# Mamba and mixture-attention sandwich on one core: the attention stage's value blocks, scores and attention passes put in another order

## What is computed

```python
q = _rope(jnp.einsum('bsd,hdp->bhsp', x, Wq))
k = _rope(jnp.einsum('bsd,hdp->bhsp', x, Wk))
gv = _gate(x, Wsel_v)
v = jnp.einsum('bsd,bhse,hedp->bhsp', x, gv, Wv)
att = jax.nn.softmax(jnp.einsum('bhsp,bhtp->bhst', q, k) / np.sqrt(P), axis=-1)
o = jnp.einsum('bhst,bhtp->bhsp', att, v)
go = _gate(x, Wsel_o)
return jnp.einsum('bhsp,bhse,hepd->bsd', o, go, Wo)
```

## Time and profile before

| what | value |
|---|---|
| median of 3 runs | 4357.75 us (4352.01 to 4357.77) |
| the profiled execution's own time | 4360.78 us |
| its span, first to last instruction | 4358.8 us |
| TensorE busy | 3803.9 us (87%) |
| VectorE busy | 3630.8 us (83%) |
| GpSimd busy | 2849.6 us (65%) |
| ScalarE busy | 2029.6 us (47%) |
| mean granted TensorE clock | 0.909 |

### The profile page before, as it was taken

One profiled execution on the slowest core, in us unless ns is written; L12 is line 12 of the kernel. 1 busy time (PEld: TensorE's weight loads), 2 busy tenths in 40 slices (PEclk: granted clock), 3 DMA queues, 4 the chain that ended last, 5 costly groups with the idle time before them and its releaser, 6 DMA issues. The chain is left out here.

```text
span 4358.8 us, 54031 instructions
## 1 busy us (share of the span) xinstructions
PE 3803.9 (87%) x15744; PEld 2541.1 (58%) x15744; DVE 3630.8 (83%) x4012; ACT 2029.6 (47%) x3761; POOL 2849.6 (65%) x2524
## 2 busy tenths in 40 slices
PE   6777867867765599999999999999999999999787
PEld 2233323323322377777777777777777777777676
DVE  5999999999998478877887887887888788778598
ACT  4544535535443244544444444444444444444433
POOL 2758668567594366766766766766766766766444
PEclk8877877877876799999999999999999999999898
DMA  1000000000000300100100100100100100000101
GB/s 39 0 10 15 24 5 19 24 5 19 15 5 20 131 13 12 41 14 10 41 14 10 41 14 10 41 14 10 41 14 10 41 14 10 20 14 15 31 29 44
DMA packets 48726, 97.83 MB, mean 22 GB/s; under 512 B 3570, under 2 KB 33138, under 8 KB 46228
## 3 DMA queue, kind: packets, MB, share of 16 engines
q1 hardware_dynamic: 47620, 92.94, 6.2%
q0 software_dynamic: 1040, 4.19, 0.2%
HBM read 80.34 MB, written 16.78 MB: 22 GB/s over the span
## 5 line engine op out<-in xcount | busy, mean ns | idle before, releaser
L702 DVE TENSOR_TENSOR_SCAN state<-dA,dBx 128x2048 f32<-128x2048 f32 x128 | 726.8, 5678 | 25.9 <-POOL y_part L289 21.3
L1234 ACT ACTIVATE prob<-ps_b,negmax 128x512 f32<-128x512 f32 x512 | 346.1, 687 | 652.3 <-DVE negmax L1353 652.3
L286 POOL TENSOR_TENSOR state<-state,c_copy 128x1024 f32<-128x1024 f32 x120 | 345.5, 2879 | 374.8 <-DVE state L702 374.8
L1347 DVE TENSOR_TENSOR vg<-ps_b,gates 128x1024 f32<-128x1024 f32 x256 | 313.5, 1224 | 253.1 <-PE ps_b L1072 241.1
L961 POOL TENSOR_TENSOR qk_full<-vg 128x512 f32<-128x512 f32 x256 | 329.0, 1285 | 253.3 <-DVE vg L1347 253.3
L549 ACT ACTIVATE dA<-dt,a_neg 128x511 f32<-128x511 f32 x512 | 326.9, 711 | 323.9 <-DVE state L702 323.7
L974 POOL TENSOR_TENSOR ogT_low<-prob,ogT_high 128x512 fp32r<-128x512 f32 x256 | 324.0, 1295 | 208.9 <-ACT ogT_high L1267 208.9
L372 PE MATMUL ps_a<-xp_high,ident_r 33*128 33x512 f32 x256 | 163.0, 637 | 332.6 <-DVE dBx L692 307.9
L1070 PE MATMUL ps_b<-ogT_high,wo_high 128*128 128x512 f32 x1024 | 413.2, 403 | 11.1 <-DVE ogT_low L1399 10.8
L1070 PE MATMUL ps_b<-wv_high,xT_high 128*128 128x512 f32 x1024 | 414.6, 405 | 0.0
L289 POOL TENSOR_TENSOR y_part<-y_part,state 128x1024 f32<-128x1024 f32 x120 | 403.4, 3362 | 9.4
(11 more groups left out here) (237 smaller groups left out, 9530.9 us busy)
## 6 DMA issues: line engine op xcount, KB each, us to landing
xT<-xT_scratch SPq DMA_DIRECT2D x65, 512.0 KB, 3.3
wv<-in_wv SPq DMA_DIRECT2D x8, 1024.0 KB, 4.9
wo<-in_wo SPq DMA_DIRECT2D x8, 1024.0 KB, 7.0
x_in<-in_x SPq DMA_DIRECT2D x8, 512.0 KB, 4.7
x_a<-in_x SPq DMA_DIRECT2D x8, 512.0 KB, 5.3
x_scratch<-x_a SPq DMA_DIRECT2D x8, 512.0 KB, 2.9
xT_scratch<-x2T SPq DMA_DIRECT2D x8, 512.0 KB, 2.6
scores_scratch<-sg SPq DMA_DIRECT2D x8, 512.0 KB, 3.5
```

Of the source, the lines that this page charges most:

```text
L286: pool.tensor_tensor(state, state, c, ALU.mult).then_inc(hc_part_done, 1)
L702: dve.tensor_tensor_scan(h[n % 2][:, :, :].rearrange("p c s -> p (c s)"), dA[n % 2][:, :, :].rearrange("p c s -> p (c s)"), dBx[n % 2][:, ...
L1234: act.activation(prob[h][:, t, :], ps[:, score_bank(t) + h, :], ACT.Exp, bias=negmax[:, t, h:h + 1], accum_out=total[:, h, t:t + 1]).then_ ...
```

## The change

It does five things in stage B.

1. TensorE: `scores(2)` and `scores(3)` stand ahead of `values(1, 0)`, and `values(1, 3)` stands behind the first head's transposes.
2. TensorE: `attend` makes a head's four passes with the high probabilities first, then its four passes with the low ones. The first four wait for `pT_high` in place of `pT_low`. All eight have 128 columns: `vv` now holds low values, high values and zeros, and the low pass takes the high values and the zeros. `pv_psum` comes from the low passes alone. A wait for the third `gate_values` of the batch is added.
3. VectorE: `gate_values(0)` stands behind `maxima(0)` and `maxima(1)`; `gate_values(3)` behind the first head's `low_probabilities`; `add_parts(0)` behind `low_gates`.
4. `aside` is no longer a tile of its own but the second half of `qk_full`, and `rotate` waits for `oT_done`.
5. GpSimd fills the zeros of `vv` once at the start.

```diff
-        oT, aside = sb("oT", [P, S]), sb("aside", [P, S])
+        oT, aside = sb("oT", [P, S]), qk_full[:, 1, :]
...
-        vv = sb("vv", [P, 2, TT, 2 * HP], F32R)
+        vv = sb("vv", [P, 2, TT, 3 * HP], F32R)
...
             def low_values(it, h):
                 pool.wait_ge(v_high, it * 2 + h + 1)
-                pool.tensor_tensor(vv[:, h, :, HP:2 * HP], v[:, h, :, :], vv[:, h, :, 0:HP].bitcast(F32), ALU.subtract).then_inc(v_low, 1)
+                pool.tensor_tensor(vv[:, h, :, 0:HP], v[:, h, :, :], vv[:, h, :, HP:2 * HP].bitcast(F32), ALU.subtract).then_inc(v_low, 1)
...
             pool.memset(out_gate[:, :, :], 0.0).then_inc(zero_done, 1)
+            pool.memset(vv[:, :, :, 2 * HP:3 * HP].bitcast(F32), 0.0).then_inc(zero_done, 1)
...
-            def attend(it, h, c):
-
-                if c == 0:
-                    pe.wait_ge(v_low, it * 2 + h + 1)
-                n = h * TT + c
-                pe.wait_ge(pT_low, it * N + n + 1)
-                bank, last = ATTEND_BANK[h], c == TT - 1
-                if last:
-                    pe.matmul(ps[0:HP, bank, :], vv[:, h, c, 0:HP], probT[1][:, n % RING, :], start=False, stop=False)
-                mm = pe.matmul(ps[:, bank, :], vv[:, h, c, :], probT[0][:, n % RING, :], start=(c == 0), stop=last)
-                if not last:
-                    mm = pe.matmul(ps[0:HP, bank, :], vv[:, h, c, 0:HP], probT[1][:, n % RING, :], start=False, stop=False)
-                mm.then_inc(pv_psum, 1)
+            def attend(it, h):
+
+                pe.wait_ge(v_low, it * 2 + h + 1)
+                pe.wait_ge(vg_done, it * 4 + 3)
+                bank = ATTEND_BANK[h]
+                for c in range(TT):
+                    pe.wait_ge(pT_high, it * N + h * TT + c + 1)
+                    pe.matmul(ps[:, bank, :], vv[:, h, c, 0:2 * HP], probT[0][:, c % RING, :], start=(c == 0), stop=False)
+                for c in range(TT):
+                    pe.wait_ge(pT_low, it * N + h * TT + c + 1)
+                    pe.matmul(ps[:, bank, :], vv[:, h, c, HP:3 * HP], probT[1][:, c % RING, :], start=False, stop=(c == TT - 1)).then_inc(pv_psum, 1)
...
                 values(it, 0, 3)
-                values(it, 1, 0)
                 scores(it, 2)
                 scores(it, 3)
+                values(it, 1, 0)
                 values(it, 1, 1)
                 values(it, 1, 2)
-                values(it, 1, 3)
                 for n in range(TT):
                     turn_probabilities(it, n)
-                for c in range(TT):
-                    attend(it, 0, c)
+                values(it, 1, 3)
+                attend(it, 0)
                 for n in range(TT, N):
                     turn_probabilities(it, n)
                 turn_gates(it)
-                for c in range(TT):
-                    attend(it, 1, c)
+                attend(it, 1)
...
             def rotate(it):
 
                 dve.wait_ge(vsum_done, CREDIT + it * VSUM)
+                dve.wait_ge(oT_done, it * 2)
...
-                gate_values(it, j, b, 0)
                 maxima(it, 0)
                 maxima(it, 1)
+                gate_values(it, j, b, 0)
                 gate_values(it, j, b, 1)
                 maxima(it, 2)
                 maxima(it, 3)
                 gate_values(it, j, b, 2)
-                gate_values(it, j, b, 3)
                 for n in range(TT):
                     low_probabilities(it, n)
+                gate_values(it, j, b, 3)
                 output_gates(it)
                 if more or more_pairs:
                     tops(*coming, 0)
-                add_parts(it, 0)
                 for n in range(TT, N):
                     low_probabilities(it, n)
                 low_gates(it)
+                add_parts(it, 0)
                 add_parts(it, 1)
```

More of the change, by code:

```diff
@@ L1205, in _ @@
             pe.wait_ge(consts_done, 1)
+            pe.wait_ge(zero_done, 2)
             turns(pe, start, batch)
@@ L1238, in high_values @@
                 act.wait_ge(vsum_done, CREDIT + it * VSUM + h * 6 + 6)
-                act.activation(vv[:, h, :, 0:HP], v[:, h, :, :], ACT.Copy).then_inc(v_high, 1)
+                act.activation(vv[:, h, :, HP:2 * HP], v[:, h, :, :], ACT.Copy).then_inc(v_high, 1)
             def high_probabilities(it, n):
@@ L1472, in _ @@
             dve.wait_ge(consts_done, 1)
-            dve.wait_ge(zero_done, 1)
+            dve.wait_ge(zero_done, 2)
             turns(dve, start, batch)
```

## The result

| | before | changed |
|---|---|---|
| median, same chip | 4354.9 us (4352.01 to 4357.77, 4 runs) | 4574.02 us (4572.49 to 4577.11, 4 runs) |
| span of the profiled execution | 4358.8 us | 4572.0 us |
| its own time | 4360.78 us | 4573.94 us |
| mean granted clock over the span | 0.909 | 0.896 |

The changed kernel is slower by a factor of 1.0504, with a 95% interval of 1.0486 to 1.0522. 4594 was predicted, with a range of 4537 to 4663.

A forecast was written before the change was run, and what follows sets the result against it. TensorE, busy 2516.7 of 2555 us, was taken as the bound, at 40.4 us a batch. Profiled 4360.8 + 211 (batches) + 5 (pair changes) + 20 (clock) - 3 (to the median) = 4594 us, range 4537 to 4663.

The forecast's parts named there:

- Second wait: TensorE before the second head's attention: the late fourth `gate_values` delays sums, `high_values` and rounded blocks; 2.3 us of waiting.
- First wait: TensorE before the first transpose: the last exponential stands behind `high_values(0)`, delayed by the late first `gate_values`; 0.82 us idle.
- rival 1: The wait before the first transpose does not come, as GpSimd's sums run closer together; 2.5 us a batch, 4540 us; chance 0.08.
- Third move: `add_parts(0)` behind `low_gates` holds up `move_part(1)`; `gate_outputs` starts at 3011.59 instead of 3008.28, the output product at 3015.00.
- 3.3 us a batch: Lengthening of each stage B batch, read at the output product's start, 3015.00 instead of 3011.69; 211 us over 64 batches.
- Changes of pair: `low_wqk`, 1.30 us, between the first head's sums delays the first transpose; at most 9 us, less absorbed waits, taken as +5.
- The granted clock: Clock falls in many batches behind the wait before the second head's attention; 0 to 1.1 us a batch, 0.3 taken, 20 us.
- Edits at nothing: Wider low passes, moved scores, later ring freeing, `aside` and `rotate`'s wait, and zeros were taken to cost nothing.
- The sum: Whole kernel: 4360.8 + 211 + 5 + 20 - 3 = 4594 us.
- Rival 2: Clock low for most of the attention, transposes not counting as busy; 147 us in place of 20, 4721 us; chance 0.05.
- Rival 3: Faster: TensorE's own order alone counts, so each batch loses its 1.2 us of waits; 77 us, 4281 us; chance 0.03.
- Rival 4: No change: the new waits just eat the 1.2 us a batch won by grouping; 4358 us; chance 0.01.

The follow-up runs named there:

- e1: The change with `values(1, 3)` back ahead of the first head's transposes and the fourth `gate_values` back ahead of its remainders: 4418.2 us.
- e4: The kernel before with only `values(1, 3)` moved behind the first head's transposes and the fourth `gate_values` behind its remainders: 4551.1 us.
- e2: The change with the first `gate_values` put back ahead of the first two `maxima`: 4528.9 us.
- e3: The change with the first `add_parts` put back ahead of the second head's remainders: 4555.9 us.
- e5: e3 with six extra matmuls into an unread bank between `turn_gates` and the second head's attention, to hold the clock up: 4523.0 us.
- e9: The change with `values(1, 3)` put back on TensorE alone; the fourth `gate_values` stays behind the remainders on VectorE: 4611.0 us.
- e7: The kernel before with all passes 128 columns wide, interleaved as before, without the grouping or the moves: 4360.1 us.
- e12: e6 with `scores(2)` and `scores(3)` ahead of `values(1, 0)`, as the change has them: 4348.3 us.
- e6: The change with all moves of VectorE's and TensorE's lists undone, leaving the grouped passes and their equal width: 4344.5 us.
- e10: The change with only the fourth `gate_values` put back ahead of the remainders on VectorE; `values(1, 3)` stays behind the transposes: 4569.6 us.
- e8: e6 with `move_part(0)` behind `high_gates`, `add_parts(0)` late as in the change, and `move_part(1)` not waiting for `add_parts(0)`: 4328.6 us.
- e11: The change with six extra matmuls into an unread bank before the second head's attention, to hold the clock up: 4576.2 us.

## Why the prediction was right, and where its sizes were off

The direction, the mechanism and the size held: 4574 against 4594. Point by point:

- **Second wait, the fourth `gate_values` late.** Right. 2.3 us were predicted and 1.96 measured. From the first transpose to the second head's attention it is 2954.67 - 2945.30 = 9.37 us, and the working gives 3006.41 - 2997.00 = 9.41. The wait is shorter since TensorE's own steps in between took 7.41 us rather than 7.12: the value block behind the transposes 1.47 (1.36 taken), 20 transposes 2.35 (2.19 taken). That sum and wait trade against each other, and the batch's end does not feel it. e1 and e4 show this move to be the largest cost: 156 of 219 us come back with it, 195 come with it alone.
- **First wait, the first `gate_values` behind two `maxima`.** Right in place and releaser, a bit too long: 0.82 predicted, 0.51 measured in the batch shown. Two small things make the 0.31. From the end of the first `gate_values` to the first transpose it is 2945.30 - 2938.80 = 6.50 us, where the working has 2997.00 - 2990.36 = 6.64: the two sums and what follows them run closer together than I added them; rival 1 said so, but took the wait to vanish. And TensorE itself comes later: it is free 9.49 us behind the start of the `maxima` (2944.79 - 2935.30), where the working has 2996.18 - 2986.86 = 9.32. e2 puts the move at 45 us.
- **Third move, `add_parts(0)`.** Right by the timeline: `gate_outputs` starts 14.65 us behind the first transpose (14.59 worked), 2.04 behind the start of `spread_gates` (about 2 named), and the output product 3.40 behind that (3.41). One detail was wrong: the first `add_parts` does not overlap `low_gates`, but starts 0.03 us behind its end. e3 and e5 show that the move costs 0.70 us a batch only where the clock holds.
- **3.3 us a batch.** 3.07 measured at full clock (43.21 - 40.15). From the first transpose to the output product the batch shown takes 18.05 us, worked 18.00; what is missing is the shorter first wait.
- **Changes of pair, +5 and 0 to 9 as bounds.** Mis-sized: the 15 distances there grew by 63.8 us, where 3.18 us each, as in ordinary batches, makes 47.7. So they cost 16 us more, above my bound. The price of `low_wqk` held: where it stands in the batch, the first wait is 1.75 in place of 0.51 us, seven times 1.24 or 9 us, and with the first `gate_values` early (e2) it is gone. The term that I left out is the other stop on the same path, `wo_low` in the first batch of a pair: the first wait grew from some 0.35 to 1.83 us there, where an ordinary batch got 0.51, and the 7 distances that hold it grew by 4.05 us in place of 3.18, another 6.
- **The granted clock, +20.** It falls as I thought, behind the second wait, in 33 of 48 ordinary batches, and is back before the output product. But such a batch is only 0.17 us longer, so some 5 to 10 us in all. The reason given, that the stretch lies under other waits, held where `add_parts` is late and the stretch lies behind the second wait: 0.17 us in the change, 0.14 in e2, 0.23 in e9 (against only 3 batches at full clock). With `add_parts` early a low batch costs 0.92 us (e3), in e4 1.04, close to the upper end of 1.1. The step that failed is that I added 0.3 us of clock a batch on top of the late `add_parts`; the two overlap.
- **Edits at nothing.** The width is one (e7). The scores' move is one in ordinary batches (39.91 us in e12, 39.96 in e6), but not across a change of pair: 43.11 us against 42.21, 6 us in all. In e12 TensorE waits for exponentials at `scores`, 8.3 us in 14 times, which the working had ruled out for an ordinary batch; in the change itself no such wait is in the view.
- **The sum.** 63 distances x 3.07 make 193, the low stretches of ordinary batches 5, and what the 15 distances at changes of pair have beyond 3.07 each 18, together 216 as measured in stage B; predicted were 211 + 20 + 5. That 4594 came so near is in part luck: clock and batch were taken some 30 us too high together, and the changes of pair, 11 too low, took part of it back.
- **Rival 2,** low for most of the attention, did not occur: in the batch shown the clock stays 1.00 throughout, and where it falls, it does so for some 3.4 us and behind the 2 us of waiting. The rule of the Trainium skill (TensorE: Matmul & The Clock Gate, Part 4: PE-mode transpose) that a transpose does not count as busy is not borne out in the change: none of the low stretches of its stage B touches a transpose, and in e1, with the same transposes and without the second wait, no ordinary batch has a low stretch. In e10 the stretches do lie under the second head's transposes, but behind a wait of 1.05 us; whether the transposes have a part in that, no run tells.
- **Rival 3,** a gain of 77 us by grouping, did not occur, and its price was wrong as well: even with nothing moved (e6) grouping is worth 11 us. The chain of sums, `high_values`, `move_part` and blocks sets when the second head's remainders start, and so when `spread_gates` does. I had named that chain as fitting "with almost nothing to spare", and did not carry it on to the rival's price. Where the chain is shortened as well (e8), 26 us are won.
- **Rival 4,** no change, would have needed the second wait to vanish.

What is left are the 62 us by which e1 is above before. It holds the late first `gate_values` and the late `add_parts` without the value block's move; its ordinary batch takes 40.98 us against 39.91 in e12. No run takes them apart, but the traces do for one batch of each. In e1 (first transpose at 2907.11) `gate_outputs` starts 11.61 us behind the first transpose, in e12 (2871.42) 10.52. Of that 1.09 us, 0.28 is there when the second head's remainders start (6.31 against 6.03), since GpSimd, which got the first `gate_values` later, ends its last sum later. The other 0.81 comes behind `low_gates`, where the first `add_parts`, ScalarE's second `move_part` and the second `add_parts` stand in a row.

Not settled: why some batches have a low stretch and others with the same lists have none, and whether the grouping would do as well with the narrow low pass.

## What to carry to other kernels

When a step is moved back on one engine, follow the longest chain that starts at its consumer on the next engine (here gating, sums, rounded values, a copy, rounded blocks): a move of 1.2 us of VectorE work that looks like a filled gap put 2 us of idleness into each of 64 batches. Such a producer and its consumer must be moved in both lists or in none, and putting back one of them alone may be worth nothing, or cost. Two costs that lie at the same time do not add up: undoing either shows little, and only the two-by-two table shows both.

## What the runs showed of the hardware

- **A low clock that costs nearly nothing.** The stretches of about 3.4 us at 0.50 behind a 2 us wait cost 0.14 to 0.23 us a batch when the engines behind TensorE were late anyway (the change, e2, e9), and 0.92 to 1.04 us when not (e3, e4). In the change they come in 33 of 48 batches with the same lists and the same 2 us wait. Such a wait is not needed: in e10 a wait of 1.05 us precedes them, in 19 of 48. In the kernel before, whose waits for remainders are 0.24 us in the batch shown, none of the 48 has one. A few matmuls into a bank that nobody reads, laid in the wait, keep the clock at 1.00 (e5, e11), and gain only where the low clock is exposed.
- **A small VectorE instruction up to five times as long beside GpSimd.** `out_gate` multiplies 128x64 with two operands from SBUF. Before, 57 of its 128 instructions overlap none of GpSimd's and take 0.21 us each; the 71 others take 0.22 to 0.76. In the changed kernel all 128 overlap one, and take up to 1.30. Its rows (ns min/median/max), before and then changed:

```profile
L1361 DVE TENSOR_TENSOR out_gate<-gates,share x128: 211/259/761, 1508.3 to 4051.8; 128x64 f32<-128x64 f32 x128
```

```profile
L1360 DVE TENSOR_TENSOR out_gate<-gates,share x128: 210/752/1295, 1503.5 to 4264.4; 128x64 f32<-128x64 f32 x128
```

In the batch shown two of them take 1.43 us from 2950.38, beside GpSimd's sum from 2950.31 to 2951.59; in the change nothing waits for it, in e9 it is the wait of 28.4 us above. `gate_values`, one operand of which comes from PSUM, takes 1.21 to 1.23 us in either kernel and is not drawn out. The Trainium skill (SBUF — State Buffer, Terms) says that VectorE and GpSimd share one pair of ports, which an instruction holds to its end while the other engine is fully blocked. The durations here agree with it.
